# A token-mixing and expert kernel on one core: shorter first Toeplitz loads, and other places for three weight pieces and a bias

## The reference, cut to what matters

```python
h = embed(x)                                   # table row, then a 384x256 projection, times 16
n = layernorm(h)
x1 = silu(depthwise_conv3(n @ w1.T + w1_b))    # 256 channels
y  = ssm(x1, A, B, C, D)                       # linear recurrence over the sequence, per channel
h  = h + (y * silu(n @ v1.T + v1_b)) @ w2.T + w2_b
n2 = layernorm(h)
h  = h + (shared_expert(n2) + (expert_a(n2) + expert_b(n2)) / 2) / 2
```

## Time and profile before

| what | value |
|---|---|
| median of 3 runs | 444.79 us |
| the profiled execution, its time | 444.33 us |
| its span, first to last instruction | 442.4 us |
| PE busy | 399.5 us (90%) |
| PEld (weight loads) busy | 350.9 us (79%) |
| DVE busy | 281.8 us (64%) |
| ACT busy | 242.5 us (55%) |
| POOL busy | 213.1 us (48%) |
| DMA, mean over the span | 88 GB/s |
| share of the chain that ended last | PE 67%, DVE 17%, ACT 6%, DMA 3% |

### The profile page before, as it was taken

How to read it: one execution, slowest core, us unless ns; L and a number is a source line. 1 busy time by engine, 2 the same in 40 slices (tenths; PEclk the granted TensorE clock), 3 DMA queues, 4 the chain that set the end, 5 groups by cost and what they waited for, 6 DMA issues and landing times.

```text
span 442.4 us, 8454 instructions
## 1 busy us (share of the span) xinstructions
PE 399.5 (90%) x2880; PEld 350.9 (79%) x2880; DVE 281.8 (64%) x608; ACT 242.5 (55%) x435; POOL 213.1 (48%) x235
## 2 busy tenths in 40 slices
PE   3878899899998864799999999999999999998996
PEld 2767788888678762598898998988988988887885
DVE  6668998989655779866556465565554554655333
ACT  4675778778886335544544645635635635535442
POOL 7769998821008256547446337247247237333000
PEclk9999999999998989799999999999999999999999
DMA  2442121259799972100121021111201301100101
GB/s 63 122 148 95 43 66 52 73 166 305 220 309 282 254 273 84 50 0 3 54 90 46 31 68 48 53 42 47 80 15 48 92 3 48 47 0 0 49 0 47
DMA packets 32779, 38.86 MB, mean 88 GB/s; under 512 B 3461, under 2 KB 29027, under 8 KB 32624
## 3 DMA queue, kind: packets, MB, share of 16 engines
q1 hardware_dynamic: 29616, 32.99, 24.6%
q0 software_dynamic: 3136, 5.52, 4.2%
HBM read 34.56 MB, written 8.65 MB: 98 GB/s over the span
## 4 chain that ended last, share of the span: by engine, by line
PE 67%; DVE 17%; ACT 6%; issue 4%; DMA 3%; POOL 1%; DVEq 0%; ACTq 0%; POOLq 0%; SPq 0%
PE ps L1139 20%; PE ps L1140 20%; PE ps L1141 20%; DVE hid_lo L1070 3%; DMA toep_l<-kernel_rows_dram 2%; DVE stat L948 2%; PE ps L1222 2%; PE ps L1177 2%; PE ps L1258 1%; DVE h2n L961 1%; DVE sw_lo L1017 1%; PE ps L1147 1%; DVE catT_lo L941 1%; DVE act_out L1064 1%; DVE hnT L990 1%
## 5 line engine op out<-in xcount | busy, mean ns | idle before, releaser
L1070 DVE SCALAR_TENSOR_TENSOR hid_lo<-act_out,hid_hi 128x512 fp32r<-128x512 f32 x64 | 56.2, 879 | 56.6 <-ACT hid_hi L855 56.6
L842 ACT ACTIVATE act_out<-ps,vec 128x512 f32<-128x512 f32 x32 | 22.1, 689 | 91.4 <-PE ps L1141 91.4
L1064 DVE SCALAR_TENSOR_TENSOR act_out<-ps,vec,act_out 128x512 f32<-128x512 f32 x32 | 24.0, 750 | 53.4 <-ACT act_out L842 53.4
L667 POOL TENSOR_TENSOR h_sb<-h_sb,bias_e 128x256 f32<-128x256 f32 x32 | 24.4, 766 | 53.4 <-DVE h2n L961 53.4
L1140 PE MATMUL ps<-h2nT_lo,sw_hi 128*128 128x512 f32 x128 | 50.0, 391 | 0.0
L1141 PE MATMUL ps<-h2nT_hi,sw_lo 128*128 128x512 f32 x128 | 50.0, 391 | 0.0
L1139 PE MATMUL ps<-h2nT_hi,sw_hi 128*128 128x512 f32 x128 | 49.9, 390 | 0.0
L660 POOL TENSOR_TENSOR zc_lo<-v_sb,zc_hi 128x256 fp32r<-128x256 f32 x32 | 29.6, 924 | 34.9 <-ACT zc_hi L832 34.9
L846 ACT ACTIVATE act_out<-ps,vec 128x512 f32<-128x512 f32 x32 | 22.1, 689 | 41.1 <-PE ps L1141 41.0
L527 POOL DMA_INDIRECT cat<-table_dram,x_ids x32 | 36.4, 1139 | 8.2 <-issue 5.8
L855 ACT ACTIVATE hid_hi<-act_out 128x512 fp32r<-128x512 f32 x64 | 39.7, 622 | 0.0
(11 more groups left out here) (133 smaller groups left out, 1261.9 us busy)
## 6 DMA issues: line engine op xcount, KB each, us to landing
toep_l<-kernel_rows_dram SPq DMA_DIRECT2D x14, 512.0 KB, 9.3
toep_r<-kernel_rows_dram SPq DMA_DIRECT2D x12, 512.0 KB, 6.7
h_rows_dram<-h_ring SPq DMA_DIRECT2D x32, 128.0 KB, 1.9
h_in<-h_rows_dram SPq DMA_DIRECT2D x8, 512.0 KB, 4.5
stage<-w_e_dram POOLq DMA_DIRECT2D x7, 512.0 KB, 3.7
out_dram<-o_sb SPq DMA_DIRECT2D x7, 512.0 KB, 3.2
bias_e<-rows_dram SPq DMA_DIRECT2D x1, 1024.0 KB, 6.8
toep_r<-kernel_rows_dram SPq DMA_DIRECT2D x4, 256.0 KB, 7.6
```

The source lines that it names most:

```text
L667: nc.gpsimd.tensor_tensor(at, at, bias_e[:, bass.ds(e, 1), :].rearrange("p o c -> p (o c)"), ALU.add).then_inc(h2_biased, 1)
L842: nc.scalar.activation(act_out[:, n % 4, :], ps[bank][:, :], ACT.Silu, bias=vec[:, C_SB1 + j:C_SB1 + j + 1]).then_inc(act_done, 1)
L1064: nc.vector.scalar_tensor_tensor(act_out[:, n % 4, :], ps[bank + 1][:, :], vec[:, C_SB3 + j:C_SB3 + j + 1], act_out[:, n % 4, :], ALU.add, ...
L1070: nc.vector.scalar_tensor_tensor(hid_lo[:, n % 4, :], act_out[:, n % 4, :], 0.5 if kind == SHARED else 0.25, f32(hid_hi[:, n % 4, :]), ALU ...
```

## The change

The first loads of the six `toep_l` slots (q = 4 to 9) also skip the zero quarter. POOL fills it: after stage A it waits for what SP waits for, and sets the first half of the row in all partitions of a slot to zero, six `memset`s of 1024 words per partition. SP waits for each before it issues that slot's two loads. Piece 0 is loaded at 12 us, into an unused part of `toep_r`; ACT rounds it at the end of group 0 (after step 7's `hn`), POOL subtracts at the start of group 3, and SP waits for that before it loads q = 3 over it. Piece 7, which shared a buffer with piece 0, no longer waits. `add_w2_bias(1, 1)` moves from behind the four `power_step`s to behind `add_w2_bias(0, 1)`, ahead of `piece_lo(1)`. `piece_lo(8)` moves from ahead of POOL's wait for DVE's pieces into `mixer_1`, behind two `mixer_lo` and two `mixer_bias`.

```diff
@@ -109,6 +109,7 @@
     raw_a = flat[:, raw_at:raw_at + (KC + 4) * D]
+    raw_w2 = flat[:, raw_at + (KC + 5) * D:raw_at + (KC + 7) * D]
     k_sum = flat[:, raw_at + (KC + 4) * D:raw_at + (KC + 5) * D].rearrange("p (h t) -> p h t", t=SEQ)
@@ -216,6 +217,7 @@
     toep_in = [sem(f"toep_in{s}") for s in range(TRING)]
+    low_zero = sem("low_zero")
     ssm_done = sem("ssm_done")
@@ -387,13 +389,13 @@
     free = o_sb[:, :, :, :].rearrange("p a g c -> p (a g c)")
-    raws = [stage[:, 0, :], stage[:, 2:4, :], stage[:, 1, :]] + [free[:, n * BLK:(n + 1) * BLK] for n in range(4)]
+    raws = [raw_w2, stage[:, 2:4, :], stage[:, 1, :]] + [free[:, n * BLK:(n + 1) * BLK] for n in range(4)]
     raws += [stage[:, 0, :], stage[:, 2:4, :]]
...
     sources = [w_b[:, 0, :], w_e[RES - 1]] + [w_b[:, n, :] for n in range(1, 7)] + [w_e[0]]
-    LO_BY = (0, 1, 0, 0, 0, 0, 0, 0, 1)
+    LO_BY = (1, 1, 0, 0, 0, 0, 0, 0, 1)
     PIECES = [(raws[n], his[n], los[n], piece_sem[n], 16, LO_BY[n], LO_BY[:n + 1].count(LO_BY[n]), sources[n])
@@ -425,13 +427,20 @@
-            toep_part(q, 0, HALF if q >= TRING else 0)
+            if TRIGHT <= q < TRING:
+                sp.wait_ge(low_zero, q - TRIGHT + 1)
+            toep_part(q, 0, HALF if q >= TRIGHT else 0)
             toep_part(q, 1, 0)
+        def piece_in(n):
+            raw, _, _, signal, _, _, _, src = PIECES[n]
+            sp.dma_start(raw, src).then_inc(signal, 16)
...
                 sp.dma_start(raw_a[:, KC * D:], w_a[:, KC * D:]).then_inc(wa_in, 16)
+                piece_in(0)
         sp.dma_start(bias_row[:, 0:1, :], bass.AP(rows.tensor, D, [[0, P], [D, 1], [1, D]])).then_inc(rows_in, 16)
@@ -442,6 +451,8 @@
                 sp.wait_ge(wv_lo_done, 2)
+            if r == 1 + TRIGHT:
+                sp.wait_ge(w_lo_done[1], 1)
             if 2 <= r < 2 + TRIGHT:
@@ -464,10 +475,6 @@
-        def piece_in(n):
-            raw, _, _, signal, _, _, _, src = PIECES[n]
-            sp.dma_start(raw, src).then_inc(signal, 16)
         def piece_used(n):
@@ -476,15 +483,12 @@
         sp.dma_start(w2_bias, bass.AP(rows.tensor, 0, [[0, P], [D, 1], [1, D]])).then_inc(rows_in, 16)
-        piece_in(0)
         piece_in(1)
...
         sp.wait_ge(ssm_done, 2 * NQ)
-        for n in range(3, 7):
+        for n in range(3, 8):
             piece_in(n)
-        piece_used(0)
-        piece_in(7)
         piece_used(1)
@@ -590,9 +594,16 @@
+        def piece_lo(n):
+            src, hi, lo, _, _, _, _, _ = PIECES[n]
+            pool.wait_ge(w_hi_done, n + 1)
+            nc.gpsimd.tensor_tensor(lo, src, f32(hi), ALU.subtract).then_inc(w_lo_done[1], 1)
         def group(i):
...
             for r in range(RES):
+                if i == GROUPS - 1 and r == 0:
+                    piece_lo(0)
                 if r % 2 == 0 and (r or i):
@@ -620,6 +631,15 @@
         power_pair(RES * GROUPS - 2, (RES - 2) % 4)
+        pool.wait_ge(hn_turned, 4 * GROUPS)
+        pool.wait_ge(catT_lo_done, RES * GROUPS)
+        for s in range(4):
+            pool.wait_ge(h_stored[s], 16 * 2 * GROUPS)
+        for q in range(TRIGHT, TRING):
+            if q == TRIGHT + 4:
+                pool.wait_ge(mm_done, 8 * (GROUPS - 1))
+            never = toep(q)[:, :, 0:HALF, :, :].rearrange("p j t c w -> p j (t c w)").bitcast(F32)
+            nc.gpsimd.memset(never, 0.0).then_inc(low_zero, 1)
@@ -672,6 +692,7 @@
                 mixer_bias(0, 0, g)
+            piece_lo(8)
             for g in range(GROUPS):
@@ -710,20 +731,14 @@
-        def piece_lo(n):
-            src, hi, lo, _, _, _, _, _ = PIECES[n]
-            pool.wait_ge(w_hi_done, n + 1)
-            nc.gpsimd.tensor_tensor(lo, src, f32(hi), ALU.subtract).then_inc(w_lo_done[1], 1)
         pool.wait_ge(rows_in, 48)
         add_w2_bias(0, 1)
+        add_w2_bias(1, 1)
         piece_lo(1)
...
             power_step(g, g, eps2_done, rstd2_done)
-        add_w2_bias(1, 1)
-        piece_lo(8)
         pool.wait_ge(w_lo_done[0], LO_BY.count(0))
@@ -742,6 +757,11 @@
         nc.scalar.copy(proj_hi[:, :, :].rearrange("p k n -> p (k n)"), raw_a[:, 0:KC * D]).then_inc(wa_hi, 1)
+        def piece_hi(n):
+            src, hi, _, signal, count, _, _, _ = PIECES[n]
+            act.wait_ge(signal, count)
+            nc.scalar.copy(hi, src).then_inc(w_hi_done, 1)
@@ -767,6 +787,8 @@
                                  scale=rstd[:, r % 4:r % 4 + 1]).then_inc(hn_first, 1)
+            if r == 7:
+                piece_hi(0)
             if r == 5:
@@ -805,12 +827,6 @@
-        def piece_hi(n):
-            src, hi, _, signal, count, _, _, _ = PIECES[n]
-            act.wait_ge(signal, count)
-            nc.scalar.copy(hi, src).then_inc(w_hi_done, 1)
         for q in range(NQ):
@@ -820,7 +836,6 @@
                 nc.scalar.copy(y_at(q, bank), y_part(q, bank, 1)).then_inc(y_low, 1)
-        piece_hi(0)
         act.wait_ge(ssm_done, 2 * NQ)
@@ -1102,8 +1117,6 @@
             z_part(u)
-            if u == 9:
-                piece_lo(0)
         for g in range(GROUPS):
@@ -1331,7 +1344,7 @@
             y_turn(u)
-        pe.wait_ge(w_lo_done[0], 1)
+        pe.wait_ge(w_lo_done[1], 1)
         for g in range(GROUPS):
...
```

## The result

The changed kernel took **442.72 us** (median of 20 runs, 440.86 to 443.98); the kernel before, on the same chip, 444.70 us. The ratio is 0.9953, 95% interval 0.9940 to 0.9966: faster by 2.1 us (1.5 to 2.7), where 5.8 were forecast, and above the upper end of the range, 442.0.

What follows compares the result with a forecast made beforehand. Stage C is PE's own work, so its start, mixer_mm(1, 0) at 184.44 us, is the yardstick. Seam -6.0, loads -0.3, stage A +0.5 sum to -5.8 us: 439.0 us against the median 444.79, range 436.8 to 442.0.

Steps and rivals of the forecast that it cites:

- The stream: Toeplitz loads up to stage B: the stream ends about 2 us earlier, of which PE can use 0.27; gain 0.3 us.
- End by about 162.5, before the first `zc_lo` is due: POOL in the seam: two bias additions and piece_lo(1), started at about 155, are done in time.
- second rival: Load stream not relieved, POOL becomes the bound in the seam: +2.7 us, 441.7 us; chance 0.13.
- The unlocked `h2n` and `sw_lo`: DVE in the seam: without POOL's addition and piece_lo(8) beside them, they take 1.95 and 2.0 us less.
- Piece 0 in stage A: ACT's rounding costs 0; POOL's 1.29 us subtraction before a power step costs 0.5 us (bounds 0 and 1.3).
- fourth rival: Stage A pays in full for both halves of piece 0, 1.9 us in place of 0.5: 440.4 us; chance 0.08.
- PE's path: Seam: PE's first layer starts at 173.7, twelve matmuls take 4.74 us, so mixer_mm(1, 0) at 178.4; gain 6.0 us.
- first rival: PE's clock stays low for longer over its first layers in the seam: +1.5 us, 440.5 us; chance 0.12.
- The memsets: POOL, after stage A: six of 0.97 us each; SP's first load 1.0 us later, no cost taken for DVE's convolution.
- The rule that I weighed: DVE instructions with two SBUF inputs contend with POOL ones that read SBUF, not with ones that only write: memsets cost nothing.
- the rival that ended slower: Memsets of 2.4 us each lock DVE's convolution out until 126.8, 9.6 us behind 117.28: 448.6 us; chance 0.04.
- `piece_lo(8)` in slot 0: Start of stage C: POOL's 2.37 us there has more than a microsecond of slack behind it; cost 0.

Runs made afterwards that it cites:

- e9: The kernel before with only the move of piece 0 (load, rounding, subtraction, SP's wait): 441.91 us, ratio 0.9957.
- e7: The changed kernel with piece_lo(0) at step 2 of group 3, behind POOL's kernel_step, in place of step 0: 440.83 us, ratio 0.9924.
- e1: The changed kernel without the skipped quarter: whole first toep_l loads, no memsets or waits for them: 442.44 us, ratio 0.9958 to the kernel before.
- e3: The changed kernel with piece_lo(0) at step 4 of group 3, behind POOL's kernel_step, in place of step 0: 443.02 us, ratio 0.9964.
- e5: The changed kernel with the second bias addition in slot 0 behind the first mixer_lo, and piece_lo(8) two power steps later: 440.74 us, ratio 0.9921.
- e6: The changed kernel with whole first loads, piece_lo(0) at step 2 of group 3 and the second bias addition in slot 0: 438.00 us, ratio 0.9858.
- e8: The changed kernel with the second bias addition back behind the four power steps: 442.00 us, ratio 0.9960 to the kernel before.
- e12: The same kernel as e6, measured once more: 439.01 us, ratio 0.9888 to the kernel before.
- e4: The kernel before with the six first toep_l loads in longer rows at equal bytes, Toeplitz values wrong: one run, 442.98 us.
- e2: The kernel before with only the skipped quarter and the memsets: 446.04 us, ratio 1.0028.
- e11: The changed kernel, quarter still skipped, with piece_lo(0) at the end of step 2 of group 3 and the second addition in slot 0: 438.20 us, ratio 0.9870.

## Why the prediction was wrong

- **The stream** is the step that failed: "a skipped quarter is worth 0.5 us in the stream, six of them 3.0 us", and so "w2's bias arrived at 157.4 before, now at about 155". The 3.1 against 3.6 us per slot were times between landings, and the halved rows did not make the difference: by packets, 1024 rows took 3.27 and 3.14 us before and 3.26 in the shortened loads, which saved 0.7 us over five slots. The memset delayed the first load by 1.1 us, close to the 1.0 forecast, and stage A by 1.3. The bias came at 159.6, 4.6 us later than the 155 that I built on, and PE waited 2.81 us for q = 15.
- **"End by about 162.5, before the first `zc_lo` is due"** fell with it. It is the second rival, with 169.1 worked out for the end of the fourth `zc_lo`; it ended at 170.1, a microsecond later again by stage A. I gave it 0.13, on the strength of one comparison of landings in two stretches that differed in more than the size of their rows. At the first power step the sum had 2.1 us won (2.31 and 0.3 less 0.5) and the trace has 1.38 lost: 3.5 of the 3.75 us by which the forecast of 5.8 was off at the yardstick. Stage A is 0.65 of them, the stream and POOL's run behind it the rest.
- **The unlocked `h2n` and `sw_lo`**: 1.95 and 2.0 us forecast, every `h2n` near 0.4 and the four `sw_lo` in 2.5 us measured, 3.43 together. Right, and 0.25 less than the sum had, since the path beyond runs over ACT's `zc_hi` (1.05 us of POOL's waiting) and no longer over POOL alone.
- **Piece 0 in stage A**: 0.5 forecast, 1.15 measured (e9, e7). The row was right (DVE waits 1.20 us), the cover was not: I took PE's slack of one product as slack of the stage. The rounding on ACT cost nothing, as forecast. This was the fourth rival's direction, at half its size.
- **PE's path** to `mixer_mm(1, 0)`: 4.74 us assumed, 5.2 to 5.3 when all twelve matmuls run without a gap (e1, e3, e5, e6, e8, e12); the first rival's mechanism. In the changed kernel it does not decide: the low level lasted 3.4 us there (176.7 to 180.1) against 6.8 before, and the first layers had a gap before `mixer_mm(1, 0)` for POOL's `zc_lo`. In those six it does.
- **The memsets**: forecast 0.97 us each and no harm to the convolution; 0.90 each, and the convolution beside them at its 0.75 us. The rule that I weighed (the Trainium skill, SBUF — State Buffer, "Who interferes with whom") held as far as these rows reach, and the rival that ended slower did not come about. Its sum was also a little high: 112.3 + 6 x 2.4 is 126.7, 9.4 us behind 117.28. The other side of the rule shows where POOL reads: the three `sw_lo`, with two SBUF inputs each, took 4.08 us beside POOL's `piece_lo(8)` and 1.89 without it.
- **`piece_lo(8)` in slot 0** cost nothing (`hid_lo` 0.74 us), as forecast.

## What to carry to other kernels

Before moving work ahead of an engine's queue, find the latest arrival that the queue starts on, and count everything from there to the hand-over: two parts that each fit in an engine's slack need not fit together, and each looks good alone. Work for which nobody waits belongs behind the first operation that releases the bottleneck. Before a load is shortened, see whether it is paid by bytes or by rows, count the packets of a stretch and not the landings in it, and do not take the price of a size from two stretches that differ in anything else.

## What the runs showed of the hardware

- Toeplitz loads with rows of 1 KB and less, DMA engines full: the queue moves 312 to 326 rows per microsecond, whether all are 1 KB or half are 512 B (before and changed kernel, 298 and 234 GB/s in the first stretch). The same 1 MB in 128 rows of 8 KB takes 2.8 us, at 365 GB/s (e4).
- A POOL operation that only writes (`memset`, 128x1024) leaves DVE's convolution steps with two SBUF inputs at 0.75 us (changed kernel, e2, e11); one that reads SBUF (the addition, 2.5 us) holds DVE's `h2n` of 0.4 us until it ends (2.43 us in before, e8 and e9).
- PE at the 1.2 GHz level (granted clock 0.50): the matmuls of the first layers follow each other every 0.43 us, and every 0.23 at full clock. In e5 the granted clock fell at 170.5, when PE had only pairs of transposes left with about a microsecond between them, and rose again at 180.7, six microseconds after the first layers had begun to run without a gap: all twelve matmuls ran at the low level. In the changed kernel it was low from 176.7 to 180.1 only (both pairs of times are worked out from windows of 2 and 5 us). What decides between the two no run here was made to tell.
